# First layer of a two-layer transformer kernel: scores twelve points behind the maxima in place of sixteen

## What is computed

```python
x = x + 0.5 * L0_ffn(layernorm(x))          # main matmul, top-2 of 8 LoRA experts
x = x + L0_attn(layernorm(x))               # 16 heads of 16, softmax over 512 keys, out projection
x = x + 0.5 * L0_ffn(layernorm(x))
x = x + 0.5 * L1_ffn(layernorm(x))          # 32 experts, top 4
x = x + L1_attn(layernorm(x))               # latent attention, causal
x = x + 0.5 * L1_ffn(layernorm(x))

# L0_attn, for each batch b and head h:
scores = q @ k.T * HEAD_DIM ** -0.5         # 512 x 512
attn = softmax(scores)
out = attn @ v
```

## Time and profile before

| | us |
|---|---|
| median of 3 runs | 1483.33 |
| lowest and highest | 1478.59, 1485.69 |
| the profiled execution, its own time | 1489.86 |
| its span in the trace | 1487.8 |
| first reduction of maxima (L914) starts | 73.7 |
| first exponential (L602) starts | 113.3 |
| last reduction of maxima ends | about 420.9 |
| last exponential ends | 452.3 |
| first scatter of the last batch's rows | 490.8 |

### The profile page before, as it was taken

One profiled execution on the slowest core, in us unless ns is written; L12 is line 12 of the kernel. 1 busy time (PEld: TensorE's weight loads), 2 busy tenths in 40 slices (PEclk: granted clock), 3 DMA queues, 4 the chain that ended last, 5 costly groups with the idle time before them and its releaser, 6 DMA issues.

```text
span 1487.8 us, 22532 instructions
## 1 busy us (share of the span) xinstructions
PE 1288.7 (87%) x6702; PEld 831.9 (56%) x6702; DVE 949.1 (64%) x2798; ACT 672.6 (45%) x1706; POOL 493.0 (33%) x495
## 2 busy tenths in 40 slices
PE   6769898898887599998769889889889997899997
PEld 4514243343335588887536455556556555778886
DVE  6786758777778322224598878887897793033334
ACT  2205655565672055553245444554554452255550
POOL 2054040052214455551211211351143143355551
PEclk7959998999999799999998999999999998899999
DMA  8627543074304276544010000020010112255647
GB/s 284 107 27 114 184 85 43 1 147 152 146 25 159 96 240 196 189 153 143 15 43 29 29 1 1 11 103 1 8 37 15 58 36 100 94 198 180 207 136 300
DMA packets 78928, 152.15 MB, mean 102 GB/s; under 512 B 11677, under 2 KB 60254, under 8 KB 75230
## 3 DMA queue, kind: packets, MB, share of 16 engines
q1 hardware_dynamic: 63022, 108.59, 25.5%
q0 software_dynamic: 15360, 41.96, 7.9%
q10 hardware_dynamic: 432, 0.17, 0.0%
HBM read 85.29 MB, written 65.01 MB: 101 GB/s over the span
## 4 chain that ended last, share of the span: by engine, by line
PE 56%; DVE 28%; ACT 6%; issue 6%; DMA 3%; POOL 1%; SPq 0%; DVEq 0%; POOLq 0%; ACTq 0%
PE m_psG L1263 12%; PE m_psY L1279 5%; DVE a_t L1713 5%; DVE a_mx L914 4%; PE a_psA L1472 3%; DVE a_nb L1721 3%; PE a_psO L478 3%; PE m_psX L1254 3%; PE a_psU L1454 3%; PE a_psU L453 3%; ACT a_pr L1583 2%; PE m_psY L161 2%; PE a_psO L1495 2%; PE a_psW L419 2%; PE a_psP L1485 2%
## 5 line engine op out<-in xcount | busy, mean ns | idle before, releaser
L166 POOL DMA_INDIRECT outs_dram<-m_ys,dest x192 | 183.9, 958 | 166.4 <-ACT m_ys L1184 152.5
L1583 ACT ACTIVATE a_pr<-a_psA,a_nb 128x512 f32<-128x512 f32 (+3 forms) x256 | 132.6, 524 | 220.2 <-DVE a_nb L1721 219.3
L1204 DVE TENSOR_TENSOR m_hm<-m_psG,m_sg 128x128 f32<-128x128 f32 x192 | 56.0, 292 | 270.1 <-ACT m_sg L1178 171.2
L1263 PE MATMUL m_psG<-arena,m_xgT 128*128 x768 | 203.6, 388 | 3.9 <-ACT m_xgT L1172 2.7
L914 DVE TENSOR_REDUCE a_mx<-a_psU 128x1 f32<-128x512 f32 x256 | 163.6, 684 | 67.5 <-PE a_psU L453 61.7
L1639 POOL TENSOR_TENSOR a_q<-a_q,a_t 64x512 f32<-64x512 f32 x64 | 80.8, 1263 | 356.5 <-DVEq L1716 336.1
L166 POOL DMA_INDIRECT rows_dram<-a_xd,slot x112 | 115.0, 1027 | 157.0 <-DVE a_xd L146 74.5
L602 ACT ACTIVATE a_P<-a_psS 128x512 f32<-128x512 f32 x256 | 142.8, 597 | 51.1 <-PE a_psS L464 44.9
L1263 PEld LDWEIGHTS m_psG<-arena,m_xgT 128*128 128x128 f32 x768 | 131.6, 191 | 20.8 <-issue 9.2
L1721 DVE TENSOR_REDUCE a_nb<-a_psA 128x1 f32<-128x512 f32 (+3 forms) x256 | 113.3, 485 | 38.1 <-PE a_psA L1474 28.5
L453 PE MATMUL a_psU<-arena 96*128 96x512 bf16 x256 | 106.1, 416 | 33.2 <-DVE a_mx L914 31.2
(11 more groups left out here) (296 smaller groups left out, 2377.4 us busy)
## 6 DMA issues: line engine op xcount, KB each, us to landing
m_xg<-rows_dram SPq DMA_DIRECT2D x46, 512.0 KB
arena<-in_mo_w SPq DMA_DIRECT2D x9, 2048.0 KB
arena<-part_dram SPq DMA_DIRECT2D x96, 128.0 KB
arena<-outs_dram SPq DMA_DIRECT2D x18, 512.0 KB, 3.9
rows_dram<-a_P SPq DMA_DIRECT2D x6, 1024.0 KB, 14.2
part_dram<-a_part SPq DMA_DIRECT2D x16, 384.0 KB, 5.4
rows_dram<-arena SPq DMA_DIRECT2D x6, 1024.0 KB, 15.0
arena<-outs_dram SPq DMA_DIRECT2D x5, 1024.0 KB, 11.1
```

The source lines that it names most:

```text
L166: pool.indirect_dma_start(out=rows_dram, out_offset=bass.IndirectOffsetOnAxis(ap=slot[:, c:c + 1], axis=0), in_=row, in_offset=None).then_ ...
L1263: ins = pe.matmul(psG[b % 2][:, 0:2 * INTER], xgT[:, (b % 2) * D + k * P:(b % 2) * D + (k + 1) * P], GU[:, ds(e * (KD * 2 * INTER) + k * 2 ...
L1583: ins = act.activation(pr[S % 2][:, AT[t]:AT[t] + (t + 1) * P], psA[:, AT[t]:AT[t] + (t + 1) * P], ACT.Exp, bias=nb[S % 2][:, t:t + 1], sc ...
```

## The change

The scores of a group stand twelve points behind its maxima: a function `scored` gives, for a point, the group, the key tile and the half that are scored there. TensorE and ScalarE both use it, for the scores, the exponentials, the values and the copy of `psO`. With it the copy of `psO` moves from p % 8 == 0 to p % 8 == 4, the turn of "o" from 1, 9, 17, 25 to 5, 13, 21, 29 and its `normalise` from 2, 10, 18, 26 to 6, 14, 22, 30 (four points later in p, of a group that is one further on, so four points earlier for each group). The turn of the maxima moves from 4, 12, 20, 28 to 2, 10, 18, 26. Splitting them stays. The one-hot work of VectorE at i = 4 moves one to four points forward. No instruction is added or removed on any engine.

```diff
-    TO, NRM, SPLIT, MX = (1, 9, 17, 25), (2, 10, 18, 26), 0, (4, 12, 20, 28)
+    BEHIND = 12
+    TO, NRM, SPLIT, MX = (5, 13, 21, 29), (6, 14, 22, 30), 0, (2, 10, 18, 26)
...
+    def scored(i, p):
+
+        n = PTS * i + p - BEHIND
+        return n // 8, n // 2 % 4, n % 2
+
+    def turned_group(i, p):
+
+        return scored(i, p)[0] - 1
+
     def turn_units(i, p):
 
-        g = 4 * i + p // 8
+        g, done = 4 * i + p // 8, turned_group(i, p)
...
-        if p in TO and 0 <= g - 3 < GROUPS:
-            out.append(("o", g - 3))
+        if p in TO and 0 <= done < GROUPS:
+            out.append(("o", done))
         if p in MX and 0 <= g - 1 < GROUPS:
             out.append(("mx", g - 1))
...
-    ONES_AT = {p: (q, (n,)) for q, at in ((0, (2, 3, 4, 5)), (1, (10, 11, 12, 13))) for n, p in enumerate(at)}
+    ONES_AT = {p: (q, (n,)) for q, at in ((0, (1, 2, 3, 4)), (1, (6, 7, 8, 9))) for n, p in enumerate(at)}
     ONES_AT[OP] = (2, (0, 1, 2, 3))
-    VALUES_AT = {7: 0, 15: 1}
+    VALUES_AT = {5: 0, 10: 1}
...
                 g, kt = 4 * i + p // 8, p // 2 % 4
+                sg, st, odd = scored(i, p)
                 for n in (2 * (p % 2), 2 * (p % 2) + 1):
                     if live(g):
                         maximum(g, kt, n)
-                    if live(g - 2):
-                        score(g - 2, kt, n)
-                if p % 2 == 0 and live((4 * (g - 2) + kt - 1) // 4):
-                    values(4 * (g - 2) + kt - 1)
+                    if live(sg):
+                        score(sg, st, n)
+                if odd == 0 and live((4 * sg + st - 1) // 4):
+                    values(4 * sg + st - 1)
                 side(i, p)
...
-                if p % 8 == 0 and live(g - 3):
-                    act.wait_ge(pv_done, 4 * (g - 2))
-                    if g - 3 >= 1:
-                        turned(act, ("o", g - 4))
+                if kt == 0 and odd == 0 and live(g - 1):
+                    act.wait_ge(pv_done, 4 * g)
+                    if g - 1 >= 1:
+                        turned(act, ("o", g - 2))
                     act.copy(Osb[:, :], psO[:, :]).then_inc(o_copied, 1)
...
-                if p in NRM and live(g - 3):
-                    normalise(g - 3)
+                if p in NRM and live(turned_group(i, p)):
+                    normalise(turned_group(i, p))
```

More of the change, by code:

```diff
@@ L591, in _ @@
             for i, p in points:
-                g, kt = 4 * i + p // 8, p // 2 % 4
-                for c in (2 * (p % 2), 2 * (p % 2) + 1):
-                    if live(g - 2):
-                        st = 4 * (g - 2) + kt
+                g, kt, odd = scored(i, p)
+                for c in (2 * odd, 2 * odd + 1):
+                    if live(g):
+                        st = 4 * g + kt
                         act.wait_ge(s_ready, 4 * st + c + 1)
```

## The result

The changed kernel takes 1513.48 us (median of 4 runs, 1505.03 to 1513.68), the kernel before 1484.51 on the same chip (4 runs, 1478.59 to 1490.46). The ratio is 1.0172, 95% interval 1.014 to 1.0204: slower by 1.7%, where 0.2% had been forecast, and outside the range given.

The account below looks back on a forecast made before the run. TensorE was taken to bound the long middle part, stopped by hand-overs. Head +2.5, middle +2.9 and end -2.0 summed to +3.4 us: 1486.7 against the median 1483.33, with a range of 1478 to 1494.5.

Parts of the forecast that it names:

- Head: Points 12 to 15 of the first batch: eight scores and values blocks come in; +2.5 us, ends 1.06 and 4.7.
- Middle: Both sweeps, the one turned bank: waits removed -7.7 us, waits added +10.6, sum +2.9.
- the waits on the division: Middle: turns of x and h behind a turned "o" no longer wait for VectorE to divide; 4.5 us in 4 waits removed.
- the attention input behind "o" at p = 14: Middle, i = 1, 2: it now waits for the division of "o" turned at p = 13; 0.6 us each, +1.2.
- The five turns of the maxima behind x and h: Middle, p = 2 and p = 10: each turn waits for a ScalarE copy, 0.77 us each.
- the four of "o" behind x and h: Middle, p = 21 and p = 29 (i = 0, 1): each turn waits for a ScalarE copy, 0.77 us each.
- the attention output at p = 19: Fourth batch: it comes one point behind the maxima and waits for exponentials and the 1.86 us copy; +2.5 us.
- cut across all cases: The clock: a shifted schedule can lose or find a half-clock stretch of about 4 us; counted either way in the range.
- Copy of the maxima: ScalarE: copy moves to p = 10, covered by LoRA products, and p = 26, light as before; no net change.
- End: Scores alone, i = 4: fewer scores and values blocks, VectorE nearly full; -2.0 us, ends 0 and -5.5.
- Two ScalarE copies in a row: Slower rival, p = 2 and p = 10: copies hold ScalarE, scores stop TensorE; +10.6 us, 1493.9; 22%.
- Both ends overlap for nothing: Faster rival: head +1, end -5.5, middle -5.2 with turn waits hidden; -9.7 us, 1473.6; 12%.

Follow-up runs that it names:

- e12: The changed kernel with the turn of the maxima at p = 1, 9, 17, 25, one point after their split; 1.0003 of the kernel before.
- e1: The kernel before with only the turn of the maxima moved, to p = 2, 10, 18, 26; 1.0162 of the kernel before.
- e2: The changed kernel with the turn of the maxima one point later, at p = 3, 11, 19, 27; 1.0317 of the kernel before.
- e9: The kernel before with one of four turns of the maxima moved, to points 2, 12, 20, 28; 1.0031 of the kernel before.
- e11: The kernel before with one of four turns of the maxima moved, to points 4, 12, 20, 26; 1.0082 of the kernel before.
- e7: The changed kernel with six extra unused 128-column f32 matmuls at the end of five points of batches 1 to 3; 1.0122 of the kernel before.
- e8: The kernel before with six extra unused 128-column f32 matmuls at the end of five points of batches 1 to 3; 1.0008 of the kernel before.
- e14: The changed kernel with the maxima turned at 1, 9, 17, 25 and six extra unused matmuls at five points of batches 1 to 3; 1.003 of the kernel before.
- e13: The changed kernel with scores fourteen points behind in place of twelve and the maxima turned at 1, 9, 17, 25; 0.9987 of the kernel before.

## Why the prediction was wrong

*What bounds the kernel.* Right: TensorE in the middle, stopped by hand-overs. It was left there as a list of waits, each at its own length.

*Head: predicted +2.5, measured -0.7* (point 16 stands 38.45 us behind the first reduction, 39.16 before). The eight scores went in: TensorE was busy 10.18 of 11.20 us, at 0.73 of the clock in place of 0.50. The first exponential came at 99.9 us, near the 101 forecast. Point 16 itself, which the step had counted in, took 0.7 us longer, so that the head comes to 0.0, below even the lower end of 1.06. The denser work brought the clock, and the step chose 2.5 against it: in the seven kernels here with twelve points the low stretch ends 32.2 to 35.9 us behind the first reduction, in the eight with sixteen 36.6 to 39.4. The Trainium skill ("TensorE: Matmul & The Clock Gate", Part 1: The HAM clock gate) says just that activity releases the clock; here the trace agrees.

*Middle: predicted +2.9, measured +26.6. This is the step that failed.* Of its terms, the waits on the division fell from 4.5 to 3.1 us and not to 1.2. The two that were left, the attention input behind "o" at p = 14, were taken at 0.6 each "between 0 and 1.20" and measured up to 1.60. The five turns of the maxima behind x and h cost 3.8 us as forecast (5 times 0.77), the four of "o" behind x and h some 2.1 of 3.1 (waits of turns on x's copy 4.2 to 4.7, on h's none to 1.6), and the attention output at p = 19 about 2.05 (0.93 + 1.12) against +2.5, though its second half's wait was there before. By the terms of the sum the idle time of the stage should have grown by about 3 us; it grew by 9.9. The score waits that were taken at "no net change" grew by 2.1 (7.9 to 10.0), the waits on reductions by 3.6 (31.2 to 34.8). The larger part was not in the sum at all: 17 us of matmuls at half clock. The prediction had read such a stretch, with its price of about 4 us, and then let it "cut across all cases" at 4 us either way, as if a schedule lost and found them evenly. A change that gives TensorE some ten new waits of 0.8 to 1.6 us does not deal evenly: here it went from 5 stretches to 14. The signs of being wrong that the prediction named were score waits up by more than a few us and reductions closer together; neither came, and no sign looked at the clock.

*Copy of the maxima: predicted no net change.* Wrong, and it is the same step seen from ScalarE. At p = 2 of i = 4 nothing covered it, since there are no maxima between, and the point grew by 3.6 us. At p = 10 it grew by 1.5 to 1.7 in batches 2 to 4. The light places weren't free either: points 26 to 28 grew by 1.2 in three batches.

*End: predicted -2.0, measured +1.8,* of which 3.6 is the p = 2 just named; without it -1.8. The mechanism was right. The timeline of VectorE at the end of the changed kernel:

```profile
464.94 0.42 DVE L632 SCALAR_TENSOR_TENSOR x<-a_psW,x 128x256 f32<-128x256 f32 x1
...
489.43 1.29 DVE L793 TENSOR_TENSOR x<-a_psW,x 128x512 f32<-128x512 f32 x2
```

From the last gated row (ends 465.4) to the last exponential (475.3) are 9.9 us against 15.4, 5.5 nearer; to the end of the addition (490.7) 25.4 against 27.1, only 1.7 nearer, and without a wait before it. VectorE is the bound there, as said.

*The rivals.* "Two ScalarE copies in a row" had the direction, the places and a chance of 22%, and its price of 10.6 us was less than half of what came, because it too counted waiting and no clock. "Both ends overlap for nothing" had the direction of the two ends, and not the size: in e12, with the maxima out of the way, the head gives 0.8 us for its 1, the end 2.2 for its 5.5, and the middle 0.6 for its 5.2. The Trainium skill ("Perfetto Trace Analysis", Optimization Strategy) was named for that rival. Its advice to interleave regimes holds in e12's trace for 3.6 us of the stage and doesn't show in the kernel's time.

*The range* was made of waits at face value and 4 us of clock. With the stage's loss of 27.7 us on 1483.33 it would have had to reach 1511: 2.8 times the 9.9 us of added waiting.

The Trainium skill ("TensorE: Matmul & The Clock Gate", A second HAM failure mode: psum-queue depth-cycling) describes TensorE pausing briefly and often between groups of matmuls and the clock swinging between its levels for it. That is what the changed kernel shows, with 14 stretches in place of 5. The prediction had weighed only the part of that page that spoke for the change.

## What to carry to other kernels

Where TensorE is about 85% busy and the trace shows stretches at half clock behind pauses of 1 to 2 us, do not price an added wait on TensorE at its length alone. Here the stage grew by 2.8 times the added idle time in the changed kernel, 2.4 times in e1 and 2.1 in e2, but by only 1.2 in e9 and 1.0 in e11, in one execution each. Look for two such waits within one or two points. When one bank passes several kinds of pieces in program order, try the piece with the longest copy (here 1.86 us) where no other piece wants the bank or the copying engine, even if that is the first point after its producer, and leave its consumer time (e2 left too little): here one position decided 1.7%, four points of distance nothing. An experiment that moves one constant alone, run before the whole, would have shown it.

## What was not expected of the hardware

Useless matmuls made a stage shorter: 20 us of filling took 14.7 us off it in the profiled execution of e7, because it brought 45 us of busy time back to the full clock. In the kernel's time it is 0.5%, not clear of noise. In kernels with less half-clock time the same filling made the stage 3 us longer (e8, e14). Stretches of half clock are not bound to the place that was changed: behind the stage, where all kernels run the same instructions but for the 56 short matmuls, the part to the end took 1023.8 us in the profiled execution of before, 1020.9 after, 1014.3 in e12 and 1009.3 in e13, so a gain of 3 us in a stage can't be told in the time of the kernel.
